# Route weights of the first experts: all read as rows from DRAM instead of two of them spread by TensorE, with the code between the attention and the expert stage, the front, round 14 and the end laid anew

## The reference, cut to what matters

```python
x = x + conv_attention(ln_over_channels(x))       # per image
t = tokens(x);  n = ln(t)
feat = mean(n, axis=0)                            # over all 16 images
w = softmax(feat @ Wr + br)                       # 1024 pixels x 8 experts: the route weights
h = relu(bn1(n @ W1[e] + b1)); h = relu(bn2(h @ W2[e] + b2)); y = h @ Wo[e] + bo
t = t + sum over e of y[e] * w[:, e]
```

## Time and profile before

| | us |
|---|---|
| median of three runs (lowest, highest) | 766.15 (765.92, 766.93) |
| the profiled execution's own time | 767.22 |
| its span, first to last instruction | 765.3 |
| PE busy in it | 754.4 |
| POOL busy | 627.2 |
| DVE busy | 517.7 |
| ACT busy | 440.1 |
| mean granted TensorE clock, share of full | 0.997 |

### The profile page before, as it was taken

One profiled execution on the slowest core, in us unless ns is written; L12 is line 12 of the kernel. 1 busy time (PEld: TensorE's weight loads), 2 busy tenths in 40 slices (PEclk: granted clock), 3 DMA queues, 4 the chain that ended last, 5 costly groups with the idle time before them and its releaser, 6 DMA issues.

```text
span 765.3 us, 11855 instructions
## 1 busy us (share of the span) xinstructions
PE 754.4 (99%) x3865; PEld 618.8 (81%) x3865; DVE 517.7 (68%) x902; ACT 440.1 (58%) x616; POOL 627.2 (82%) x385
## 2 busy tenths in 40 slices
PE   8999999999999999999999999999999999999997
PEld 7888888888777788888888888888888888888886
DVE  6878888888877766666656566565666666566564
ACT  3787777878676554545545545545545545455443
POOL 6366879888986888888888888888888888888874
PEclk9999999999999999999999999999999999999999
DMA  7354454536533630303123030321304123030100
GB/s 226 124 182 165 169 177 156 187 144 222 163 116 134 229 118 20 138 1 137 59 78 137 0 137 27 110 83 54 137 0 137 39 98 131 6 137 11 45 28 29
DMA packets 27584, 82.11 MB, mean 107 GB/s; under 512 B 3168, under 2 KB 8080, under 8 KB 27552
## 3 DMA queue, kind: packets, MB, share of 16 engines
q1 hardware_dynamic: 27264, 81.60, 30.3%
q10 hardware_dynamic: 288, 0.11, 0.1%
HBM read 64.64 MB, written 17.06 MB: 107 GB/s over the span
## 4 chain that ended last, share of the span: by engine, by line
PE 90%; DVE 4%; DMA 2%; ACT 1%; issue 1%; POOL 1%; POOLq 0%; SPq 0%; DVEq 0%; ACTq 0%
PE psum L629 66%; PE psum L619 7%; PE psum L593 5%; PE psum L572 4%; PE psum L607 3%; DVE rawmax L1166 1%; PE psum L521 1%; PE psum L512 1%; DMA route_all<-route_scratch 1%; PE psum L522 1%; PE psum L523 1%; PE psum L462 1%; DMA ident<-in_ident 0%; PE psum L650 0%; POOLq L88 0%
## 5 line engine op out<-in xcount | busy, mean ns | idle before, releaser
L1176 DVE SCALAR_TENSOR_TENSOR h_lo<-psum,h_hi 128x1024 fp32r<-128x1024 f32 x128 | 156.7, 1224 | 191.3 <-ACT h_hi L940 191.1
L940 ACT ACTIVATE h_hi<-psum 128x1024 fp32r<-128x1024 f32 x128 | 131.4, 1027 | 236.1 <-PE psum L629 236.1
L1433 POOL TENSOR_TENSOR h_lo<-w_raw,h_hi 128x1024 fp32r<-128x1024 f32 x64 | 154.3, 2412 | 37.4 <-ACT h_hi L957 37.4
L629 PE MATMUL psum<-h_hi,w_hi 128*128 128x512 f32 x382 | 119.4, 394 | 1.1 <-ACT feat L945 0.6
L1197 DVE SCALAR_TENSOR_TENSOR w_raw<-psum,minus_t,route_all 128x1024 f32<-128x1024 f32 x93 | 118.6, 1275 | 0.0
L629 PE MATMUL psum<-h_lo,w_hi 128*128 128x512 f32 x382 | 118.3, 391 | 0.0
L629 PE MATMUL psum<-h_hi,w_lo 128*128 128x512 f32 x382 | 118.1, 390 | 0.0
L1433 POOL TENSOR_TENSOR xn_lo<-feat_most,xn_hi 128x1024 fp32r<-128x1024 f32 x31 | 74.7, 2408 | 34.3 <-ACT xn_hi L957 34.3
L629 PEld LDWEIGHTS psum<-h_hi,w_hi 128*128 128x128 f32 x382 | 71.4, 188 | 17.6 <-issue 1.6
L629 PEld LDWEIGHTS psum<-h_hi,w_lo 128*128 128x128 f32 x382 | 71.7, 188 | 16.4
L629 PEld LDWEIGHTS psum<-h_lo,w_hi 128*128 128x128 f32 x382 | 71.7, 188 | 15.2
(11 more groups left out here) (231 smaller groups left out, 1428.7 us busy)
## 6 DMA issues: line engine op xcount, KB each, us to landing
rows<-rows_scratch SPq DMA_DIRECT2D x16, 1024.0 KB, 7.2
x_res<-in_x SPq DMA_DIRECT2D x16, 512.0 KB, 4.7
x_scratch<-x_res SPq DMA_DIRECT2D x16, 512.0 KB, 2.7
xs_in<-x_scratch SPq DMA_DIRECT2D x16, 512.0 KB, 4.9
x_res<-x_scratch SPq DMA_DIRECT2D x16, 512.0 KB, 3.3
out<-x_res SPq DMA_DIRECT2D x15, 512.0 KB, 2.7
w_raw<-rows_scratch SPq DMA_DIRECT2D x11, 512.0 KB, 3.7
z_early<-in_x SPq DMA_DIRECT2D x8, 512.0 KB, 4.0
```

The lines of the kernel that those rows point to most:

```text
L629: mm = pe.matmul(dst[:, px], w[:, which, e, :], part[:, px], start=first and w is w_hi and part is hi, stop=last and part is lo, skip_grou ...
L940: nc.scalar.activation(h1_hi[r][:], z1[r] if src is None else src, ACT.Relu).then_inc(h1_hi_done, 1)
L1176: nc.vector.scalar_tensor_tensor(out=h1_lo[r][:], in0=z1[r] if src is None else src, scalar=0.0, in1=h1_hi[r][:].bitcast(F32), op0=ALU.max ...
L1433: nc.gpsimd.tensor_tensor(h2_lo[r][:], h2w[r], h2_hi[r][:].bitcast(F32), ALU.subtract).then_inc(h2_lo_done, 1)
```

## The change

Four places change.

- **Route weights.** The 16 spreading transposes and the semaphore `spread` go. `weigh` of slots 0 and 1 reads `route_all` like the others, and the DMAs of rows go out in the order 0 to 7. The PE places where the transposes stood hold `layer1` of slots 4 and 5 and `layer2` of slot 4; `layer1(6)` and `layer2(5)` move ahead of `layer3(4)`. `EARLY` goes from 4 to 5, with a fifth `z2_early` tile. DVE makes the low parts of slots 3, 4 and 5 first and then weighs slots 0 to 4 in a row. ACT's list is put in the same order, with `first_xs_high(1)` and the copy of the bias ahead of the first `h2_high`. POOL scales image 1's input one step earlier, and `split_low(1, 1)` stands ahead of `h2_low(0)`.
- **Start.** Five more products without a reader stand between the transposes of `wout` and the wait for the centred k weights.
- **Round 14.** DVE's `statistics` moves behind the low part of `mT` (L1073).
- **End.** `weigh` and `h2_high` of slot 127 work in two halves; the low part of slot 126 moves from POOL to DVE.

```diff
-    EARLY = 4
+    EARLY = 5
@@ z2_early
-            t[:].rearrange("p n c -> p (n c)") for t in (feat, xn2T)]
+            t[:].rearrange("p n c -> p (n c)") for t in (feat, xn2T, xT)]
@@ SP
-            for e in (2, 4, 3, 5, 6, 7, 0, 1):
+            for e in range(EXPERTS):
                 sp.dma_start(route_all[:, e, :], route_dram[e:e + 1, :].to_broadcast([128, PIXELS])).then_inc(route_loaded[e], 16)
@@ PE, layer2
-                elif at(s, EARLY + 1):
-                    pe.wait_ge(h2w_done, EARLY)
@@ PE, layer3
-                if not at(s, SLOTS - 1 + L3_LAG):
+                if at(s, SLOTS - 2 + L3_LAG):
+                    pe.wait_ge(last_low_done, 1)
+                elif not at(s, SLOTS - 1 + L3_LAG):
                     pe.wait_ge(h2_lo_done, s - L3_LAG + 1)
...
-                        pe.wait_ge(last_low_done, n + 1)
+                        pe.wait_ge(last_low_done, n + 2)
@@ PE, start
             mm.then_inc(wT_done, 1)
+            keep_running(5)
             pe.wait_ge(wk_centred, 1)
@@ PE, bridge
             pe.wait_ge(h1_lo_done, 3)
-            turn(p_k, lambda n: route[:, 0, n:n + 1].to_broadcast([128, 128])).then_inc(spread, 1)
+            layer1_into(p_k, 4)
             layer2(3, 3)
             turn_rows(IMAGES + 2, 2, p_chan[:, BANK:PIXELS])
-            turn(p_late, lambda n: route[:, 1, n:n + 1].to_broadcast([128, 128])).then_inc(spread, 1)
-            pe.wait_ge(h2w_done, 1)
-            layer1_into(p_k, 4)
+            pe.wait_ge(h1_lo_done, 4)
+            layer1_into(p_late, 5)
+            layer2(4, 4)
...
             mm.then_inc(bias_done, 1)
-            pe.wait_ge(h2w_done, 2)
-            layer1_into(p_late, 5)
-            layer2(4, 4)
+            layer1(6, 6, 0)
+            layer2(5, 5)
             layer3(4, 4, 0)
             layer3(5, 5, 0)
-            layer1(6, 6, 0)
-            layer2(5, 5)
             layer3(6, 6, 0)
@@ ACT, h2_high
-                act.wait_ge(h2w_done, s + 2 if at(s, EARLY - 1) else s + 1)
+                if at(s, SLOTS - 1):
+                    for n in range(2):
...
+                        nc.scalar.copy(h2_hi[r][:, px], h2w[r][:, px]).then_inc(h2_hi_done, 1)
+                    return
+                act.wait_ge(h2w_done, s + 1)
@@ ACT, bridge
+            z2_out(2)
             move_rows(IMAGES + 2, 0, p_chan[:, BANK:PIXELS])
-            z2_out(2)
+            h1_high(4, 4)
+            z2_out(3)
             move_rows(IMAGES + 3, 1, p_chan[:, BANK:PIXELS])
-            h2_high(0, 0)
-            z2_out(3)
-            h1_high(4, 4)
-            h2_high(1, 1)
+            h1_high(5, 5)
+            z2_out(4)
+            first_xs_high(1)
             act.wait_ge(bias_done, 1)
             nc.scalar.copy(bias_out, y).then_inc(bias_moved, 1)
-            first_xs_high(1)
-            h1_high(5, 5)
+            h2_high(0, 0)
+            h1_high(6, 6)
+            h2_high(1, 1)
             h2_high(2, 2)
-            h1_high(6, 6)
             h2_high(3, 3)
@@ DVE, rounds
-                if (n and not at(t, 1)) or at(t, IMAGES - 2):
+                if n and not at(t, 1):
                     statistics(t, slice(0 if n else 1, 2 if d else 1))
...
-                if at(t, IMAGES - 1):
+                if at(t, IMAGES - 2) or at(t, IMAGES - 1):
                     statistics(t, OF_X1)
@@ DVE, weigh
-                if at(s, 0) or at(s, 1):
-                    dve.wait_ge(spread, s + 1)
-                    weights = (p_k, p_late)[s]
-                elif isinstance(s, int) and s < EXPERTS + 2:
+                if isinstance(s, int) and s < EXPERTS:
                     dve.wait_ge(route_loaded[e], 16)
...
+                pieces = (slice(0, BANK), slice(BANK, PIXELS)) if at(s, SLOTS - 1) else (slice(0, PIXELS),)
@@ DVE, bridge
-            h1_low(3, 3)
-            weigh(0, 0)
-            weigh(1, 1)
-            h1_low(4, 4)
-            weigh(2, 2)
-            h1_low(5, 5)
-            weigh(4, 4)
-            weigh(3, 3)
+            for s in (3, 4, 5):
+                h1_low(s, s)
+            for s in range(EARLY):
+                weigh(s, s)
@@ DVE, end
+            r = (SLOTS - 2) % RING
+            dve.wait_ge(h2_hi_done, SLOTS - 1)
+            dve.wait_ge(l3_done, SLOTS - 1 - RING)
+            nc.vector.tensor_tensor(h2_lo[r][:], h2w[r], h2_hi[r][:].bitcast(F32), ALU.subtract).then_inc(last_low_done, 1)
@@ POOL, bridge and slots
             add_feature(IMAGES - 3, spare_norm)
+            scale_xs(1, 1)
             statistics(IMAGES + 2, 2, OF_X1)
             pool.wait_ge(route_done, 1)
-            scale_xs(1, 1)
             shift_xs(1, 1)
+            split_low(1, 1)
             h2_low(0, 0)
             h2_low(1, 1)
-            split_low(1, 1)
             h2_low(2, 2)
...
-                if exists(s - 2) and not at(s, SLOTS + 1):
+                if exists(s - 2) and not at(s, SLOTS) and not at(s, SLOTS + 1):
                     h2_low(s - 2, k - 2)
```

More of the change, by code:

```diff
@@ L278, in metaformer_kernel @@
         routeT_loaded = sem("routeT_loaded")
-        spread = sem("spread")
         bias_done, bias_moved, feat_most_moved = sem("bias_done"), sem("bias_moved"), sem("feat_most_moved")
@@ L954, in h2_high @@
                 r = k % RING
-                act.wait_ge(h2w_done, s + 2 if at(s, EARLY - 1) else s + 1)
+                if at(s, SLOTS - 1):
+                    for n in range(2):
+                        px = slice(BANK * n, BANK * (n + 1))
+                        act.wait_ge(h2w_done, SLOTS + n)
+                        act.wait_ge(l3_done, SLOTS - RING)
+                        nc.scalar.copy(h2_hi[r][:, px], h2w[r][:, px]).then_inc(h2_hi_done, 1)
+                    return
+                act.wait_ge(h2w_done, s + 1)
                 wait(act, l3_done, s - RING + 1)
@@ L1196, in weigh @@
                 wait(dve, h2_lo_done, s - RING + 1)
-                nc.vector.scalar_tensor_tensor(out=h2w[k % RING], in0=z, scalar=minus_t2[:, e:e + 1], in1=weights,
-                                               op0=ALU.max, op1=ALU.mult).then_inc(h2w_done, 1)
+                pieces = (slice(0, BANK), slice(BANK, PIXELS)) if at(s, SLOTS - 1) else (slice(0, PIXELS),)
+                for px in pieces:
+                    nc.vector.scalar_tensor_tensor(out=h2w[k % RING][:, px], in0=z[:, px], scalar=minus_t2[:, e:e + 1], in1=weights[:, px],
+                                                   op0=ALU.max, op1=ALU.mult).then_inc(h2w_done, 1)
             def finish(b, p):
@@ L1308, in _ @@
             slots(dve, slot)
+            r = (SLOTS - 2) % RING
+            dve.wait_ge(h2_hi_done, SLOTS - 1)
+            dve.wait_ge(l3_done, SLOTS - 1 - RING)
+            nc.vector.tensor_tensor(h2_lo[r][:], h2w[r], h2_hi[r][:].bitcast(F32), ALU.subtract).then_inc(last_low_done, 1)
             r = (SLOTS - 1) % RING
-            dve.wait_ge(h2_hi_done, SLOTS)
             for n in range(2):
                 px = slice(BANK * n, BANK * (n + 1))
+                dve.wait_ge(h2_hi_done, SLOTS + n)
                 nc.vector.tensor_tensor(h2_lo[r][:, px], h2w[r][:, px], h2_hi[r][:, px].bitcast(F32),
```

## The result

The changed kernel takes 773.14 us, the median of 5 runs (771.79 to 776.05). The kernel before took 766.93 us beside it, also 5 runs. The ratio is 1.0081, with a 95% interval of 1.0055 to 1.0107: some 6.2 us slower. The forecast was 4.2 us slower, so the sign was right and 2.0 us were missing.

The account below looks back on a forecast made before the run. The prediction took PE's list to bound the kernel. Its terms, 4.7 + 0.5 - 0.7 + 0 - 0.3 = 4.2 us, were added to 766.15 us, giving a forecast said as 770.3 us, range 767.2 to 773.2.

Parts of the forecast that it names:

- The bridge: From the route weights to `layer2(6)`: PE's unbroken piece would start 4.6 to 4.8 us later, taken as 4.7.
- the turns of DVE and POOL: In the bridge, DVE operations with two SBUF inputs and POOL operations would wait for each other, 3.4 us a pair.
- POOL's 6 us without use: In the bridge, POOL would stand six microseconds at `split_low(1, 1)`, waiting for ACT's `first_xs_high(1)`.
- PE's second and third gap: In the bridge, PE would wait 2.0 us ahead of `layer3(5)` and 2.0 us ahead of `layer3(6)`.
- The rival without turns: In the bridge DVE and POOL would not clash, so `layer2(6)` comes only 1.1 us later: 766.2 us, chance 0.09.
- The rival *faster: In the bridge POOL's first low parts come in time, PE's shorter list decides: 762.8 us; chance 0.06 including a partial version.
- The clock: PE's granted clock would fall in the bridge's gaps and slow later layers: 0 to 2.1 us, taken as 0.5 lost.
- the rival in which the clock makes it worse: Clock falls after each of the bridge's three gaps and the start gains nothing: 6.7 us slower, 772.9 us, chance 0.20.
- the forecast's own range: Whole kernel: 768.6 to 772.0 us around the forecast of 770.3, chance 0.65.
- The start: Five products fill PE's early gap and keep its clock up: 0.2 us lost to 1.3 gained, taken as 0.7 gained.
- Round 14 and the end: Earlier low part of `mT` offset by later statistics, 0; less PE waiting before slot 126's third layer, 0.3 us gained.

Follow-up runs that it names:

- the experiment with the filled gap: Changed kernel plus fifteen products without a reader in PE's gap ahead of `layer3(4)`: 773.59 us, ratio 1.0071 against the kernel before.
- the start alone: Kernel before with only the five added products without a reader at its start: 767.71 us, ratio 1.0007.
- the bridge alone: Changed kernel without the five start products, with round 14's statistics and the end as before: 772.6 us, ratio 1.0060 against the kernel before.
- the wide fill: Two wide products instead of five in the start's gap: kernel before 0.9986, with reordered bridge and new end 0.9954, changed kernel 1.0050.
- the end alone: Kernel before with only slot 127 in two halves and slot 126's low part on DVE: 766.95 us, ratio 0.9989.

## Why the prediction was right, but for one term

*The bridge.* Predicted +4.7, measured +4.53 in the changed kernel and +4.69 alone. The mechanism held step by step: the turns of DVE and POOL at 3.4 us a pair (3.3), POOL's 6 us without use (5.82), `layer3(4)` 14.25 us behind the transpose (14.05), and `layer2(6)` 24.4 (24.18). PE's second and third gap were 0.39 and 0.51 us and not 2, since the slow layers ahead of them used them up; filled they were 1.65. The rival without turns, 766.2, is out: with POOL idle the operations take 1.27 us, beside it 3.4. The rival *faster* is out too: it needed `h2_low(0)` 9.7 us behind the transpose, and PE got it at 14.05. The Trainium skill, SBUF — State Buffer (Who interferes with whom), says that a DVE instruction with two SBUF inputs contends with a GpSimd instruction that reads SBUF. The traces agree, in both directions: the `weigh` of slot 5, with one input in PSUM, took 1.27 us at 261.42, beside POOL's operation that ran from 259.24 to 262.63.

*The clock.* Predicted +0.5, measured 0. The reading that a low clock would cost something in the bridge was wrong in size: filled and unfilled gave the same. The time that was measured, 773.1, lies at the rival in which the clock makes it worse, 772.9. That rival was still wrong. Its number was hit by something else, and only the experiment with the filled gap tells the two apart. That the time still lies in the stated range, 0.06 us below its upper end of 773.2, is luck in part. It lies outside the forecast's own range (768.6 to 772.0), and 0.8 us of it is not the change's: the forecast counted from 766.15, and the kernel before took 766.93 beside the changed one.

*The start.* Predicted -0.7, with -1.3 as the bound. The mechanism held, and the size was nearer to the bound: -1.29 in the trace of the start alone, whose `ident` landed as in the kernel before. In the changed kernel's own trace it was -0.4, where `ident` came 0.8 us after PE was ready. Counted from PE's first transpose with `ident`, the transpose of rows that stands at 30.4 us in the kernel before comes 1.0 to 1.5 us sooner in all eleven traces with a fill. It does so by 1.0 us in the bridge alone too, which has no fill and whose clock didn't fall there. So what the fill saves seems to be the price of a fall of the clock, 1.0 us or more where the prediction took 0.7, and nothing where the clock holds without it.

*Where the step failed.* "Five products without a reader" were priced by their time alone. The prediction asked what they do to the clock and to the transposes behind them, and never what five more instructions do to the instruction stream. That is the missing 2 us: +2.0 at index 12. The page of before showed the instruction queues among the DMA queues, and I left them out. In the traced execution the prediction's own terms come to 4.5 + 0 - 0.4 + 0.2 - 0.4 = 3.9 us, close to the 4.2 of its sum; the 2.0 are on top.

*Round 14 and the end.* 0 and -0.3 predicted, +0.15 and -0.37 measured. Both right within what can be told.

What stays open: three of the store's packets wait for the end of q8's in the slow stores and don't in three of the stores at 20 us. That they stand behind it on one of the 16 DMA engines would fit, but the views don't name the engine of a packet, and no run separated that. And the intervals of each pair with and without the wide fill touch or overlap (1.6, 2.3 and 2.3 us better). It is the three together, with the store's length in each trace, that carry the cause, not one pair.

## What to carry to other kernels

An instruction can cost more than its time: here five more products at the start moved the packet that brings instructions behind the loop from 178 to 170 us, onto a small store on the critical chain. So when a harmless edit gains less than its mechanism gives, compare the offsets of equal events along the whole program to find where it is given back, and try the same work in fewer instructions. And when two engines that share something alternate, count them as one: move one side's inputs to PSUM or its work to where the other is idle, before shortening either list.

## What the runs showed that I had not expected

- A packet of the instruction queue in a small store: 2.80 to 3.47 us instead of 1.36, in eight traces of eight at the same place.
- With five products of 8 by 8 (ten passes) ahead of PE's wait of 1.74 us the granted clock stayed at 1.00, as with five of 128 columns, and the rounds came 1.0 us early. It is one trace.
- The clock in the start is no sure thing in a kernel without the fill: it fell to 0.50 in the kernel before and in the end alone, and did not fall in the bridge alone, with the same instructions there. PE's wait was 1.61 and 1.51 us in the first two and 1.15 in the third.
- A slow layer is free when the wait behind it ends later than it does: the stretches from 251 to 259 us at 0.50 to 0.87 cost nothing that can be measured.
- The landing of `ident` differs from one execution to the next: PE's first transpose with it starts at 4.04 to 5.33 us, and everything behind it moves along. Offsets are read from an event behind the start.
